# Attention of a hybrid block: products moved to VectorE with operands in PSUM, B's rotation moved wholly to ScalarE, and the attention laid out by halves

## The reference

```python
x = x + attn_a(layernorm(x))   # selective state-space layer, 8 heads, P = 64, N = 128
x = x + ffn(layernorm(x))      # one 128x128 ternary weight, plus a bias
x = x + attn_b(layernorm(x))   # softmax attention over the 8 entries of the first axis
x = x + ffn(layernorm(x))

# attn_a, per head and token t (B and C are rotated by a cumulated angle):
#   h = alpha_t h + beta_t Bx_{t-1} + gamma_t (u_t outer B_t);   y_t = h C_t
#   then an RMS norm over all heads and an output projection
# attn_b: q, k, v = x W + b; 16 heads of 8 features; softmax(q k^T / sqrt 8) v; output projection
```

## Time and profile before

| what | us |
|---|---|
| median of 3 runs (717.13 to 723.93) | 717.43 |
| the profiled execution | 722.47 |
| its span, first to last instruction | 720.7 |
| PE busy in the span | 565.0 (78%) |
| DVE busy | 532.6 (74%) |
| POOL busy | 531.2 (74%) |
| ACT busy | 432.8 (60%) |

### The profile page before, as it was taken

One profiled execution on the slowest core, in us unless ns is written; L12 is line 12 of the kernel. 1 busy time (PEld: TensorE's weight loads), 2 busy tenths in 40 slices (PEclk: granted clock), 3 DMA queues, 4 the chain that ended last, 5 costly groups with the idle time before them and its releaser, 6 DMA issues.

```text
span 720.7 us, 13131 instructions
## 1 busy us (share of the span) xinstructions
PE 565.0 (78%) x3872; PEld 455.1 (63%) x3872; DVE 532.6 (74%) x1006; ACT 432.8 (60%) x1244; POOL 531.2 (74%) x568
## 2 busy tenths in 40 slices
PE   4867999979996668969996668988986579686155
PEld 4746888857874556857875557876765467452144
DVE  6475878777759998765759998776679996621873
ACT  4446888877785454866775454878865348533002
POOL 5506999987769899867769898878678996321881
PEclk8887999999999889998999889999997879967569
DMA  9431132312111101222111101222211011000000
GB/s 204 141 93 53 57 92 58 105 51 65 49 50 50 50 1 49 84 66 64 51 50 49 50 2 49 86 74 77 71 50 25 26 50 46 27 3 0 1 0 29
DMA packets 53343, 39.59 MB, mean 55 GB/s; under 512 B 8339, under 2 KB 49046, under 8 KB 53270
## 3 DMA queue, kind: packets, MB, share of 16 engines
q1 hardware_dynamic: 44822, 34.51, 16.3%
q10 hardware_dynamic: 8448, 4.20, 2.0%
HBM read 33.44 MB, written 4.46 MB: 53 GB/s over the span
## 4 chain that ended last, share of the span: by engine, by line
PE 39%; POOL 22%; DVE 15%; issue 15%; ACT 7%; DMA 1%; POOLq 0%; ACTq 0%; DVEq 0%; SPq 0%
PE ps L1161 7%; POOL area L360 5%; PE ps L1315 4%; PE ps L1283 4%; PE ps L1382 4%; PE ps L1296 3%; ACT area L750 3%; DVE area L1052 2%; PE ps L1325 2%; POOL area L355 2%; POOL bn L518 2%; PE ps L1235 2%; PE ps L1372 2%; PE ps L1237 2%; PE ps L1236 2%
## 5 line engine op out<-in xcount | busy, mean ns | idle before, releaser
L713 ACT ACTIVATE turned<-ps,sct 128x128 f32<-128x128 f32 x512 | 139.4, 396 | 1.8 <-PE ps L1237 0.7
L960 DVE TENSOR_TENSOR_SCAN lmat<-arow,band 128x512 f32<-128x512 f32 x64 | 104.4, 1631 | 3.5 <-POOL band L536 2.3
L517 POOL TENSOR_TENSOR bn<-turned 128x256 f32<-128x256 f32 x64 | 62.2, 972 | 58.1 <-ACT turned L700 41.2
L700 ACT ACTIVATE turned<-ps,sct 128x128 f32<-128x128 f32 x256 | 72.9, 370 | 42.0 <-DVE turned L946 41.6
L1283 PE MATMUL ps<-cT,bT 128*128 128x128 f32 x512 | 76.6, 297 | 21.5 <-issue 12.9
L1283 PEld LDWEIGHTS ps<-cT,bT 128*128 128x128 f32 x512 | 69.0, 208 | 33.1 <-issue 32.2
L536 POOL TENSOR_TENSOR band<-bandm,sct 128x512 f32<-128x512 f32 x64 | 73.8, 1153 | 19.5 <-DMA sct<-packed 19.5
L355 POOL TENSOR_TENSOR area<-area 128x1024 f32<-128x1024 f32 x21 | 59.3, 2840 | 16.5 <-ACT area L618 13.3
L360 POOL TENSOR_TENSOR area<-area 128x1024 f32<-128x1024 f32 x28 | 70.7, 2546 | 0.6 <-DVE area L1056 0.6
L517 POOL TENSOR_TENSOR cn<-turned 128x256 f32<-128x256 f32 x64 | 49.0, 766 | 29.8 <-ACT turned L713 29.4
L618 ACT ACTIVATE area<-ps 128x256 f32<-128x256 f32 (+2 forms) x96 | 41.1, 480 | 46.2 <-PE ps L1161 31.6
(11 more groups left out here) (183 smaller groups left out, 1446.2 us busy)
## 6 DMA issues: line engine op xcount, KB each, us to landing
arow<-alpha_rows SPq DMA_DIRECT2D x32, 512.0 KB, 4.2
drow<-decay_rows SPq DMA_DIRECT2D x64, 128.0 KB, 3.1
area<-in_L_attn_a_x_dram SPq DMA_DIRECT2D x4, 512.0 KB, 6.1
xT_rows<-turned SPq DMA_DIRECT2D x4, 512.0 KB, 3.7
xt<-xT_rows SPq DMA_DIRECT2D x32, 64.0 KB, 2.5
area<-in_L_attn_a_x_dram ACTq DMA_DIRECT2D x8, 256.0 KB, 2.8
out_dram<-area ACTq DMA_DIRECT2D x8, 256.0 KB, 2.3
area<-L_attn_a_sel_proj_w_dram SPq DMA_DIRECT2D x2, 512.0 KB, 6.4
```

The costliest lines, as they stand in the source:

```text
L517: pool.tensor_tensor(out[:, 0], zc[:, 0], zs[:, 1], ALU.subtract)
L713: last = act.activation(dst[h][:, N * q:N * q + N], bank(BK_C)[:, N * q:N * q + N], ACT.Copy, scale=sct[i2][:, at + HH * h + q:at + HH * h ...
L960: dve.tensor_tensor_scan(lmat[h], arow[i2][:, HH * P * h:HH * P * (h + 1)], band[h], 0.0, ALU.mult, ALU.add).then_inc(l_dve, 1)
```

## The change

The order within a unit is kept. What changes:

- All 16 products of a chunk are VectorE's; GpSimd has none.
- The queries of a half (4 batches x 128 columns, piece Q0 or Q1) are left in the PSUM bank `BK_F[g]` and read there by the products; `exp` writes the softmax weights to the same bank, and the second products and norms read them there.
- Keys and values come in four pieces KV0 to KV3 of two batches each (a bias matmul of 512 columns and two matmuls of 256), queries in two pieces (a bias matmul of 512 columns and four of 128). ScalarE copies keys and values with two 256-column copies for each KV.
- The attention is in halves: prod0 to 3, softmax:0, exp:0, prod4 to 7 (weights and v of half 0), onorm:0, and the same for half 1 with prod8 to 15. The pairs of prod and red are spread evenly from position 63 to 86.6 (units 5 to 12).
- B is rotated wholly by ScalarE, like C: eight 128x128 instructions, no `b_cos`.
- The state's update is four 128x64 `scalar_tensor_tensor` instructions, one for each head, with no `sdec`.
- x1 is four 128x128 `scalar_tensor_tensor` instructions for a half, the constant factor being put into `w_out`.
- Three more small DMAs lay out the biases before the first unit.

```diff
-USES = [[("T", g), ("F", g), ("T", 2 + g)] + [("Q", 4 * g + s) for s in range(4)] +
-        [("T", 4 + g), ("O", g), ("T", 6 + g), ("F", 2 + g)] for g in range(2)]
+USES = [[("T", g), ("F", g), ("T", 2 + g), ("KV", 2 * g), ("KV", 2 * g + 1), ("Q", g),
+         ("T", 4 + g), ("O", g), ("T", 6 + g), ("F", 2 + g)] for g in range(2)]
...
-POOL_PRODUCTS = (1, 2, 5, 6, 7, 8, 9, 10, 12, 13, 14, 15)
-LAST_POOL_PRODUCTS = (1, 2, 4, 5, 6, 7, 8, 9, 10, 11, 12, 13, 14)
...
+         "addF0": 47.02, "load:1": 48, "var1:0": 48.01, "rs1:0": 50, "xn1:0": 50.01, "T2": 51, "rr:1": 52.02,
+         "x1:1": 53.01, "var0:1": 54.01, "rs0:1": 56, "xn0:1": 56.01, "KV0": 56.2, "kvout0": 56.3, "T1": 57,
+         "KV1": 57.02, "kvout1": 57.03, "F1": 58, "addF1": 58.01, "var1:1": 59.01, "rs1:1": 60, "xn1:1": 61.01,
+         "T3": 62, "KV2": 62.5, "kvout2": 62.6, "KV3": 62.7, "kvout3": 62.8, "Q0": 62.85, "Q1": 62.9,
+         "prod0": 63, "red0": 63.8, "prod1": 64.52, "red1": 65.32, "prod2": 66.04, "red2": 66.84, "prod3": 67.56,
+         "red3": 68.36, "softmax:0": 68.41, "exp:0": 68.56, "prod4": 69.08, "norms:0": 69.18, "red4": 69.88,
+         "prod5": 70.6, "red5": 71.4, "prod6": 72.12, "red6": 72.92, "prod7": 73.64, "red7": 74.44,
+         "onorm:0": 74.54, "prod8": 75.16, "T4": 75.46, "red8": 75.96, "O0": 76.46, "prod9": 76.68,
+         "addO0": 76.96, "var2:0": 77.06, "rs2:0": 77.46, "red9": 77.48, "prod10": 78.2, "xn2:0": 78.46,
+         "red10": 79, "T6": 79.46, "prod11": 79.72, "F2": 80.06, "red11": 80.52, "softmax:1": 80.57,
+         "addF2": 80.66, "exp:1": 80.72, "prod12": 81.24, "norms:1": 81.34, "store:0": 81.46, "red12": 82.04,
+         "prod13": 82.76, "red13": 83.56, "prod14": 84.28, "red14": 85.08, "prod15": 85.8, "red15": 86.6,
+         "onorm:1": 86.7, "T5": 87.3, "O1": 88.3, "addO1": 89.3, "var2:1": 89.4, "rs2:1": 90.3, "xn2:1": 91.3,
+         "T7": 92.3, "F3": 93.3, "addF3": 94.3, "store:1": 94.8}
...
+            def b_turn(c, k, part):
...
+                if part == 0:
+                    act.wait_ge(b_pe, n + 1)
...
+                for q in (2 * part, 2 * part + 1):
+                    for dst, at in ((bc, COS), (bs, SIN)):
+                        last = act.activation(dst[h][:, N * q:N * q + N], bank(BK_B)[:, N * q:N * q + N], ACT.Copy,
+                                              scale=sct[i2][:, at + HH * h + q:at + HH * h + q + 1])
...
+            def f_kv_out(c, q):
...
+                rows = f_bank(("KV", q), c).rearrange("p (s e) -> p s e", s=2)
+                evac(ks[:, 2 * q:2 * q + 2, :], rows[:, :, 0:D])
+                evac(vals[:, :, 2 * q:2 * q + 2].rearrange("p e s -> p s e"), rows[:, :, D:2 * D]).then_inc(f_q[q // 2], 1)
...
-                act.activation(rows, rows, ACT.Exp, scale=float(AD) ** -0.5).then_inc(f_exp[g], 1)
+                act.activation(q_bank(g), rows, ACT.Exp, scale=float(AD) ** -0.5).then_inc(f_exp[g], 1)
...
                     bT_out(c, k)
                     at_step(pieces, c, k, 0)
-                    b_sin(c, k + 1)
+                    b_turn(c, k + 1, 0)
+                    b_turn(c, k + 1, 1)
                     cT_out(c, k)
...
-                dve.tensor_tensor(sdec[:].rearrange("p (h q) -> p h q", q=PD), st, dec, ALU.mult).then_inc(sd_dve, 1)
                 dve.wait_ge(s_pe, n + 1)
                 dve.wait_ge(y_pe, n + 1)
-                dve.wait_ge(sd_dve, n + 1)
                 own = bank(BK_G).rearrange("p (h q) -> p h q", q=N)[:, :, 0:PD]
-                dve.tensor_tensor(st, sdec[:].rearrange("p (h q) -> p h q", q=PD), own, ALU.add).then_inc(s_dve, 1)
+                for q in range(HH):
+                    last = dve.scalar_tensor_tensor(st[:, q], st[:, q], sct[i2][:, CD + HH * h + q:CD + HH * h + q + 1], own[:, q],
+                                                    ALU.mult, ALU.add)
+                last.then_inc(s_dve, 1)
...
+                for q in range(4 * g, 4 * g + 4):
+                    last = dve.scalar_tensor_tensor(xres[:, q], oraw[:, q, 0:D], rr_f[:, q:q + 1], xres[:, q], ALU.mult, ALU.add)
+                last.then_inc(f_x[g], 1)
...
+                if m % NB < 4:
+                    for part in range(2):
+                        dve.wait_ge(f_q[part], 2 * c + 2)
+                    dve.wait_ge(f_pe[g], use_done(("Q", g), c))
+                    dve.tensor_tensor(prod[:, m % 2].rearrange("p (r e) -> p r e", r=NB),
+                                      q_bank(g)[:, D * q:D * q + D].unsqueeze(1).broadcast_to([P, NB, D]), ks,
+                                      ALU.mult).then_inc(f_prod, 1)
+                else:
+                    dve.wait_ge(f_exp[g], c + 1)
+                    weights = q_bank(g)[:, AH * NB * q:AH * NB * (q + 1)].rearrange("p (h r) -> p h r", r=NB)
+                    dve.tensor_tensor(prod[:, m % 2].rearrange("p (h d r) -> p h d r", r=NB, d=AD),
+                                      weights.unsqueeze(2).broadcast_to([P, AH, AD, NB]),
+                                      vals.rearrange("p (h d) r -> p h d r", d=AD), ALU.mult).then_inc(f_prod, 1)
...
+            def f_kv(c, q):
+
+                f_free(c, ("KV", q))
+                pe.matmul(f_bank(("KV", q), c), ones3[:], bias3[:, BIAS_KV:BIAS_KV + 4 * D], start=True, stop=False)
+                for r in range(2):
+                    last = pe.matmul(f_bank(("KV", q), c)[:, 2 * D * r:2 * D * r + 2 * D], xnT_f[:, 2 * q + r, :], w_qkv[:, D:3 * D],
+                                     start=False, stop=(r == 1))
+                last.then_inc(f_pe[q // 2], 1)
+
+            def f_query(c, g):
+
+                f_free(c, ("Q", g))
+                pe.matmul(q_bank(g), ones3[:], bias3[:, BIAS_Q:BIAS_Q + 4 * D], start=True, stop=False)
+                for r in range(4):
+                    last = pe.matmul(q_bank(g)[:, D * r:D * r + D], xnT_f[:, 4 * g + r, :], w_qkv[:, 0:D], start=False, stop=(r == 3))
+                last.then_inc(f_pe[g], 1)
```

147 lines of the change are left out of this document (47 added, 100 removed), and 13 rows, old and new, of the table PLACE.

## The result

The changed kernel takes 772.1 us (median of four runs; 769.4 to 774.1) where the kernel before took 718.1 beside it (717.1 to 723.9): a ratio of 1.073, 95% interval 1.066 to 1.080. The forecast was 723.4 and the range ended at 742, so it was wrong by far. The profiled executions are 769.4 and 722.5 us, their spans 767.2 and 720.7: 46.5 of the 54 us can be looked at.

A forecast was written before the change was run, and what follows sets the result against it. PE was taken as the bound in chunk 0 and units 0 to 4, VectorE in units 5 to 12. Chunk 0 +4, later chunks -3 and the tail +5 gave +6 on 717.4, so 723.4 us, range 702 to 742.

The forecast's parts named there:

- Units 0 to 4: Later chunks: four pieces in one slot of unit 4, 4.4 us of PE plus 2 of waits: +6 (+2 to +11).
- Chunk 0: Chunk without attention: B's rotation makes ScalarE the bound, 0.5 us a pair over eight pairs: +4 (0 to +11).
- Units 5 to 12: Attention units of later chunks: VectorE's work falls from 79.4 to 78.0 us, stage -9 (-13 to +1), chunk 3 -6.
- The fused state: Units 5 to 12: state update as four 64-column instructions takes 5 to 7 us in place of 9.2: -3.
- The cosines: Units 5 to 12: B's cosine products leave VectorE: -5.0 us.
- the term of -3.5: Units 5 to 12: scans, average 1.81 us against a median of 1.53, shorten with no GpSimd product beside them: -3.5.
- Its upper bound: Units 5 to 12: +1 us if products stay at 1.58 us.
- Units 13 to 15: Later chunks' last units: T5, O1, var2:1, addO1 and ScalarE's extra work, mostly hidden by idle PE: +1 (0 to +4).
- The tail: After the last chunk's units: VectorE work 47.7 us against 38.3, less earlier start and store wait: +5 (+2 to +8).
- Relief: Rival: VectorE's relief wins, units 5 to 12 fall by 12, chunk 0 +2, tail +3: 703 us; chance 0.28.
- ScalarE's bound: Rival: ScalarE's rotation bounds the projection units, chunk 0 +9, later chunks +12 in all, tail +5: 743 us; chance 0.22.
- PSUM operands not sparing VectorE: Rival: products stay at 1.58 us beside GpSimd, +7 a chunk in three chunks: 744 us; chance 0.05.

The follow-up runs named there:

- e15: Changed kernel with KV2, KV3, Q0 and Q1 still in one slot, but slot 63 in place of 62, and prod0 with them: 751.6 us, 1.045.
- e5: Changed kernel with transposes that nobody reads added on TensorE ahead of KV2's and KV3's waits in unit 4: 750.6 us, 1.043.
- e10: Changed kernel with half 0's keys, values and queries early (KV0 at slot 52, KV1 at 54, Q0 at 59): 767.7 us, 1.063.
- e7: Changed kernel with the attention products' small operand read from SBUF in place of PSUM (computes other numbers): 774.0 us, 1.074.
- e13: Kernel before with only the state's update fused into four 64-column instructions: 718.9 us beside 722.7, 0.994.
- e3: Changed kernel with the cosines of B's rotation back on VectorE and only the sines on ScalarE: 777.0 us, 1.078.
- e4: Kernel before with only B's rotation moved wholly to ScalarE, no cosines on VectorE: 741.2 us, 1.030.
- e17: Kernel before with all sixteen products of a chunk on VectorE, none on GpSimd, both operands in SBUF: 750.9 us, 1.047.
- e2: Changed kernel with KV2, KV3, Q0 and Q1 spread over slots 63 to 66 and the attention's steps pushed together into 65.6 to 86.6: 752.1 us, 1.045.
- e16: Kernel before with T5, O1, addO1, var2:1, xn2:1, T7 and F3 at the places the change gives them: 751.2 us, 1.047.
- e8: Changed kernel with x1 as before, two instructions for a half through a temporary in place of four: 768.9 us, 1.070.
- e1: Changed kernel with the last chunk's filler transposes issued before T4's and T5's wait for the attention's norm: 760.9 us, 1.059.
- e11: Changed kernel with half 0's pieces early, KV2 at 62.5, KV3 at 63.5, Q1 at 65, attention pushed together, tail transposes ahead of the wait: 750.0 us, 1.037.
- e12: The kernel of e11 with three tiles' worth of transposes that nobody reads added ahead of KV2's wait: 741.3 us, 1.028.
- e14: The kernel of e11 with KV2 at 63, KV3 at 64, Q1 at 66 and the attention from 65.6, each a slot later: 741.0 us, 1.030.

## Why the prediction was wrong

**Units 0 to 4, the step that failed.** The prediction saw the slot ("4.4 us of PE in the stage that PE bounds", T3's copy behind the rotation and the square, prod0 behind Q0) and then wrote "I take 2 us of waits: +6". It measured +17.2 / +14.5 / +12.9, beyond its bound of +11 in all three chunks; this term alone is 27 of the 40 us of error. Three steps of it failed.

- The waits are 3.8 us on PE, not 2, and they were taken as a sum instead of as a delay of the queue: PE's queue is in order, so everything of unit 5 stood behind them (e15: 5 to 7 us for one slot).
- The work was priced too low twice. A piece has 512 columns where the batch of the earlier trace rows has 384, so four of them at full clock are 5.6 us (1.41 from Q0 to Q1 in e5) and not 4.4. And the clock, which the term leaves out, fell after the idle time: 2.54 us for a piece, some 8.8 for the four, and 4 to 5 us a chunk off when filler keeps it up (e5).
- The pieces of one batch had stood apart, in slots of their own; as a price I used their busy time alone. That they had filled holes there is not shown: with half 0's pieces early again (e10) unit 2 to 3 falls to 10.0, but the time barely moves.

The prediction's mark, VectorE idle for 5 us or more ahead of prod0, was met with 7.5.

**Chunk 0: right.** A pair takes 12.43 us with ScalarE busy for 12.05, 97% (12.4 and above 95% were forecast). From unit 0 to unit 13 the chunk is 3.3 us longer, near the 0.5 a pair booked; the last two units give back 1.3, which no term had. The Trainium skill's price (ScalarE: Activation LUTs, on what ACT_TABLE_LOAD costs) would have made a pair 12.7 and the term +6; the trace disagrees.

**Units 5 to 12: the sum right, -8.9 / -9.0 / -6.8 against -9, -9 and -6, and partly by luck.** 79.9 us with VectorE at 93% (81 and 96% forecast), busy 74.7, not 78.0. Products take 1.22, as said; that the PSUM operand does it holds only for a small part (e7). The fused state was booked at -3 and gives -1.1 by itself (e13); the four instructions last 0.85 us together, where the Trainium skill (VectorE: DVE Perf Modes, the errata on a fixed latency) gave an estimate of 0.77. The prediction's warning, that the update ends later behind PE, is no loss that e13 shows. The cosines were booked at -5; undone in the new kernel they cost +2.0 / +0.2 / +1.4, and taken away in the old one they gain nothing (e3, e4). Scans fell to 1.34 us, further than the term of -3.5 needs. Its upper bound is a slip: products at 1.58 give -1.5 by its own numbers, not +1.

The parts that were run alone don't add up to the stage. Sixteen products on VectorE cost +9.0 (e17), state and cosines give back 1 to 3, and the stage still is 9 shorter. So by this estimate some 15 us a chunk come from what no run takes alone: pieces that left the stage for unit 4 and for units 13 to 15, for which the sum has -1.7, and the longer stretch of the attention. Part of it is work moved and not saved. With the four pieces back in units 5 and 6 (e2) the stage is only 4.8 / 3.0 / 0.7 below the kernel before. How the rest divides stays open.

**Units 13 to 15: +3.7 / +3.0 / +3.8 against +1.** "6 us of PE idle that hides most" failed: e16 puts the loss on half 1's last pieces, which are a chain of PE, ScalarE and VectorE and don't fit into idle time by its sum. Also x1, taken to save VectorE a microsecond, costs it more: 19.4 us over the whole trace where it was 17.0. What that is worth stays undecided (e8).

**The tail: +12.4 against +5.** The product phase was booked at 47.7 us and takes 52.0, from 695.29 to the end of the last reduction; 4.6 of that is addO0 behind the transposes, and with them out of the way (e1) it takes 47.9. So its size was right but for that. Its parts are not all tested: e17 gives +4.4 for the products alone, so an estimate from e17's 42.6 and e1's 47.9 puts the other 5 us on the order by halves. The first product came 3.8 us earlier (1.5 booked), which is not shown to be the change's: in e17, where nothing ahead of it was changed, it is 4.2 earlier. The last norm's wait for the store is gone, but T5 is 4.5 late. The step that failed is one I did not have: past which wait a queue's filler instructions are moved when the bank's last reader changes. It is worth e1's 8.8 us, more than the whole miss of 7.4.

**The rivals.** Relief had units 5 to 12 at -12 and did not come. ScalarE's bound had the right sign and the wrong cause (e3). PSUM operands not sparing VectorE did not come, since products take 1.22; but its premise, a GpSimd as full as before, was gone with the change itself.

## What to carry to other kernels

In an in-order queue, a step that waits for another engine holds up everything behind it, so put independent work of one copy's length between a producer and its consumer; e15 is such a slot and nothing else. Price a chain by where its waits stand in the queue, not by their sum. Merging small steps into large ones saves instructions, but it also puts waits and work together that had stood apart. On TensorE a hole can be paid a second time: here 2.8 us of it were followed by work at half clock in the same place of each of the three chunks. When a buffer's last reader changes, go through every wait that is derived from it, also those ahead of filler.

## What the runs showed that was not expected

- 2.8 us of idle time on TensorE in an otherwise full stage were followed by about 6 us at 1.2 GHz (e11), and 16 transposes that nobody reads took 4 to 5 us a chunk off (e5). No lower clock followed 3.0 us of idle time in chunk 0 of the kernel before.
- Less work for VectorE made the kernel before 3% slower when ScalarE got it (e4): VectorE and GpSimd were full together, and GpSimd waited 2.4 us longer for ScalarE's B in units 5 to 12 of chunk 1.
- A 128x1024 product on VectorE takes 1.22 us with an operand in PSUM. From SBUF alone it takes 1.21 to 1.22 beside an idle GpSimd (e17's tail), 1.25 to 1.37 beside one that is half busy (e7, e17), and 1.58 beside one busy for 87%.
- With e1, e2 and x1's two instructions together (e9) the kernel came to 746.4 us, 1.037, where 738 was expected if the gains add. The best forms of the changed kernel are e12 at 1.028 and e14 at 1.030, so the change as a whole stays above the kernel before.
